# Moving an offset shift from TensorE to four small transfers, with norm and offset convolution one step earlier

## The chip, the cores and the metric

The kernel runs on one core of a Trainium2 chip. The metric is the time of one execution in microseconds (us). TensorE (PE) multiplies matrices, and its weight loads are listed apart (PEld); VectorE is DVE, ScalarE is ACT, GpSimd is POOL; SyncE (SP) issues transfers, and so does ACT's queue here (SPq and ACTq in the profile).

## The reference, cut to what matters

The program is two "metaformer" layers on x of 4 images, 128 channels, 128 x 128 pixels. Only the first part is touched here, a deformable 3 x 3 convolution of the channel-normalised input:

```python
offset = _offset_conv(x, w_off)                 # 3x3 convolution, 18 channels: dy, dx of 9 taps
py = base_y.astype(x.dtype)[None] + dy
px = base_x.astype(x.dtype)[None] + dx
sampled = _bilinear_gather(x, py, px)
return jnp.einsum('bckhw,ock->bohw', sampled, w_conv.reshape(O, C, K * K))
...
x = x + _L0_conv_ref(_ln_c(x), L0_conv_w_off, L0_conv_w_conv)
```

The rest (two expert layers, a spectral convolution) is the same in both kernels.

## The kernel before, in words

`phase_a` computes this convolution. A group G is four image rows; there are 128 groups (`NG`). `order_a` writes out by hand, in slots, a list of stages that all engines walk through in the same order, each picking its own stages. A step s is 12 slots (18 at the end of an image, where six rows instead of four are sampled). In one step the stages belong to different groups: F = s+4 is loaded, transposed and normalised and gets its offset convolution, Z = s+2 gets its offsets, N = s+1 its bilinear weights, a quad of four rows is sampled, and s-2 gets the output convolution. The names that matter:

- `turn` (PE, L350) transposes the group's rows into PSUM bank 4; `stats` (DVE, L496 and L499) takes mean and variance from there; `scale` (POOL, L562 to L568) makes the scale and bias `rs`; `norm` (ACT, L437) writes the normalised rows `a_tn`; `norm_out` (ACT's queue, L446) sends them to memory, from where SP fetches windows `a_win`.
- `conv` (PE, L361) multiplies by the offset weights into banks 5 and 6, two rows at a time (`h` 0 and 1); `y_out` (ACT, L464) scales the result into the ring `a_yr`, with four activations or five, five where rows wrap in the ring.
- `zsum` (POOL, L589, L595) adds over the three tap rows and gives `a_zz` with three tap columns; `shift` (PE, L374) moves the outer tap columns by one pixel, which is one partition, by multiplying with two shift matrices into bank 6; `offs` (DVE, L517) adds the middle column and writes the offsets `a_on`.
- `offs_out` (ACT's queue, L450) stores them; `place` and `hats` (POOL, L623 or L631, L607, L610) spread them; `bend` (ACT, L473), `clip` (DVE, L528), `prod` (DVE L536, POOL L576) and `turn_s` (DVE, L545) make the weights `a_tt`.
- `sample` (PE, L405) multiplies windows by weights in three thirds. The first and the last third write banks 0 to 3, the second writes banks 4 to 7. So before the second third PE waits until norm, stats, y_out, offs and residual have read what these banks held:

```python
w.wait_ge(normed, convs)
w.wait_ge(mv_ready, convs // 2)
w.wait_ge(y_ready, 2 * convs)
w.wait_ge(on_ready, shifts)
w.wait_ge(x1_ready, outs)
```

- `evict` (ACT L482, DVE L509) copies each third out; `out` (PE, L423) is the output convolution in nine taps; `residual` (DVE, L551) adds the input.

POOL takes the stages of a step in the order prod, zsum, prod, place, hats, scale. ACT takes the three evicts, offs_out, bend, norm, norm_out, y_out. Each engine does its own in that order whatever is ready.

Of the kernel before, what the change touches and what calls it, by code (L numbers as in the profile page):

```python
# [46 lines left out]
def setup_phase(nc, ctx, ins, k):  # L47
# [5 lines left out]
    with nc.Block() as block:  # L53
# [17 lines left out]
        @block.sync  # L71
        def _(e):
            e.dma_start(k["wraw"][:, :], ins["wof"][:, :]).then_inc(w_in, 16)
            e.dma_start(k["ident"][:, :], ins["ident"][:, :]).then_inc(loaded, 16)
            e.dma_start(k["shift"][:, :, :], ins["shift"][:, :, :]).then_inc(loaded, 16)
# [3 lines left out]
            e.wait_ge(loaded, 80)  # L79
            e.wait_ge(w_in, 16)  # L80
# [10 lines left out]
NX, NTN, NYR, NOC = 10, 3, 12, 32  # L91
# [69 lines left out]
def order_a():  # L161
# [16 lines left out]
    end = t0  # L178
    for s in range(-4, NG + 3):
        t0 = steps[s]  # L180
        F, Z, N = s + 4, s + 2, s + 1
        if s == -4:
            for G in range(3):
                put(t0, "load", G)
            put(t0, "border", 0)
# [4 lines left out]
        if 3 <= s + 7 < NG:  # L190
            put(t0 + 6, "load", s + 7)
# [9 lines left out]
        if 0 <= Z < NG:  # L201
            put(t0 + 4, "shift", Z)
            put(t0 + 4, "offs", Z)
        if 0 <= F < NG:
            put(t0 + 4, "turn", F)
            put(t0 + 4, "stats", F)
            put(t0 + 6, "scale", F)
            put(t0 + 5, "conv", F, 0)
            put(t0 + 6, "conv", F, 1)
            put(t0 + 7, "norm", F, 0)  # L210
# [33 lines left out]
def phase_a(nc, ctx, ins, k, xtp, offd, x1d):  # L244
# [6 lines left out]
    zz = S("a_zz", [128, 2, 4, 3, 18])  # L251
# [12 lines left out]
    OF = SB[:, 6, 324:396].rearrange("p (r f) -> p r f", r=4)  # L264
# [4 lines left out]
    def sem(name):  # L269
# [4 lines left out]
    turned, convolved, shifted, sampled, conv_out = (  # L274
        sem(n) for n in ("turned", "convolved", "shifted", "sampled", "conv_out"))
# [3 lines left out]

    filled, bn_done, mv_ready, on_ready, reached, clipped, weighed_dve, turned_s, x1_ready = (  # L280
# [51 lines left out]
    def tensor(e):  # L332
        w = Once(e)

        convs = shifts = outs = taken = 0
# [6 lines left out]
        for o in order:  # L342
# [9 lines left out]
            elif o[0] == "conv":  # L352
# [3 lines left out]
                if h:  # L356

                    w.wait_ge(on_ready, shifts)
# [5 lines left out]
            elif o[0] == "shift":  # L364
                G = o[1]
                bank_free()
                w.wait_ge(z_step, z_count[G])

                w.wait_ge(on_ready, G)
                w.wait_ge(y_ready, 2 * convs)  # L370
                shifts += 1

                for kx in (0, 2):
                    t = e.matmul(OF[:, :, :], k["shift"][:, kx, :], zz[:, G % 2, :, kx, :], start=(kx == 0),  # L374
                                 stop=(kx == 2))
                t.then_inc(shifted, 1)
            elif o[0] == "sample":
# [8 lines left out]
                for h in range(3):  # L386
                    if h == 1:
# [4 lines left out]
                        w.wait_ge(on_ready, shifts)  # L392
# [36 lines left out]
    def scalar(e):  # L429
        w = Once(e)  # L430
        for o in order:
# [20 lines left out]
            elif o[0] == "y_out":  # L452
                _, G, h = o
                b, q = divmod(G, GI)
                for r in (2 * h, 2 * h + 1):
# [12 lines left out]
                    a.then_inc(y_ready, 1)  # L468
            elif o[0] == "bend":
# [15 lines left out]
    def vector(e):  # L485
        w = Once(e)
        e.memset(oc[:, :], 0.0)
        e.memset(sx[:, :, :, :], 0.0)
        e.memset(tt[:, :, 2304:2306], 0.0).then_inc(filled, 1)
        for o in order:  # L490
# [20 lines left out]
            elif o[0] == "offs":  # L511
                G = o[1]
                w.wait_ge(shifted, G + 1)
# [3 lines left out]
                e.tensor_tensor(on[:, G % 2, :, :], OF[:, :, :], zz[:, G % 2, :, 1, :], ALU.add).then_inc(on_ready, 1)  # L517
# [35 lines left out]
    def gpsimd(e):  # L553
        w = Once(e)
        for o in order:
# [24 lines left out]
            elif o[0] == "zsum":  # L580
                G = o[1]
                q = G % GI
                v = yr[:, 4 * G % NYR * 162:(4 * G % NYR + 4) * 162].rearrange("p (r k f) -> p r k f", r=4, k=3)
                z = zz[:, G % 2, :, :, :].rearrange("p r k f -> p r (k f)")
# [1187 lines left out]
def program(nc, ins, out, dbg):  # L1772
    with ExitStack() as ctx:
# [38 lines left out]
def constants():  # L1812
    ident = np.eye(128, dtype=np.float32)
    shift = np.zeros((128, 3, 128), np.float32)
    for kx in range(3):
        x = np.arange(max(0, 1 - kx), min(128, 129 - kx))
        shift[x + kx - 1, kx, x] = 1.0
# [20 lines left out]
    return {"io": io, "pick": pick, "rev": rev, "ident": ident, "shift": shift, "cx": np.ascontiguousarray(cx), "cy": np.ascontiguousarray(cy), "base": base, "far": far}  # L1838
# [41 lines left out]
```

## Time and profile before

| | us |
|---|---|
| median of 3 runs | 3873.46 (3870.35 to 3874.3) |
| profiled execution, its own time | 3877.71 |
| its span, first to last instruction | 3875.7 |
| PE busy | 3679.2 (95%) |
| DVE busy | 2944.7 (76%) |
| ACT busy | 1570.9 (41%) |
| POOL busy | 1474.4 (38%) |

The mean granted TensorE clock was 0.956 of full speed. The span is the time between the first and the last instruction of the profile; the profiled execution is one of several, so its time differs a little from the median. Phase A ends near 1990 us of the span; a busy share says nothing of who is waited for, so the rows further down are taken from single steps of that phase. Overlapping matmuls are counted once in a busy time.

### The profile page before, as it was taken

The numbers are of one execution on the slowest core, as the hardware profiler recorded it, in microseconds if no ns is written. First come the engines' busy times: TensorE is split into PE (matmuls) and PEld (weight loads), VectorE is DVE, ScalarE is ACT, GpSimd is POOL, SyncE is SP. The second block draws the span as 40 slices with busy tenths as digits, with TensorE's granted clock in tenths as the row PEclk, the third lists the DMA queues.
The fourth block names the chain that finished last, engine by engine and source line by source line (L and its number), as shares of the span: only waits on it lengthen the run. The fifth ranks groups of instructions, "written<-read, shape, count | busy, mean of one in ns | idle before, by whom it ended". The sixth has DMA issues, their size and how long they took to land. (4 is left out here: it accounts for less than half of the span.)

```text
span 3875.7 us, 89814 instructions
## 1 busy us (share of the span) xinstructions
PE 3679.2 (95%) x31511; PEld 2470.7 (64%) x31511; DVE 2944.7 (76%) x9687; ACT 1570.9 (41%) x4565; POOL 1474.4 (38%) x2661
## 2 busy tenths in 40 slices
PE   6999999999999999999979999999999999996667
PEld 5777777777777777777745666666666666654444
DVE  4666666666666666666648999999999999996633
ACT  3444444444444444444411444434343443434224
POOL 4444444444454444444412333333333333333210
PEclk7999999999999999999979999999999999997755
DMA  5655555555555555555527777777777777884789
GB/s 109 108 95 108 100 95 97 96 108 104 91 99 95 108 103 94 96 97 97 88 81 265 270 275 274 272 268 273 277 271 275 267 276 273 285 303 158 268 312 393
DMA packets 611250, 709.81 MB, mean 183 GB/s; under 512 B 62208, under 2 KB 493824, under 8 KB 594416
## 3 DMA queue, kind: packets, MB, share of 16 engines
q1 hardware_dynamic: 505328, 630.10, 58.3%
q10 hardware_dynamic: 104448, 71.85, 6.0%
q8 instruction: 253, 4.15, 0.5%
q14 instruction: 197, 1.61, 0.2%
q0 software_dynamic: 1024, 2.10, 0.2%
HBM read 521.26 MB, written 181.50 MB: 181 GB/s over the span
## 5 line engine op out<-in xcount | busy, mean ns | idle before, releaser
L423 PE MATMUL a_sb<-a_sr,wcv 128*128 128x512 f32 (+3 forms) x2820 | 1052.2, 515 | 0.8 <-DVE a_xo L551 0.8
L405 PEld LDWEIGHTS a_sb<-a_tt,a_win 32*128 32x128 f32 x19008 | 647.0, 186 | 116.3 <-issue 115.5
L423 PEld LDWEIGHTS a_sb<-a_sr,wcv 128*128 128x128 f32 x2820 | 493.1, 190 | 333.9 <-issue 289.1
L405 PE MATMUL a_sb<-a_tt,a_win 32*128 32x144 f32 x19008 | 679.8, 295 | 17.5 <-ACT a_yr L464 11.0
L1171 DVE TENSOR_TENSOR b_P<-b_P,b_x 128x1024 f32<-128x1024 f32 x512 | 620.1, 1212 | 0.0
L509 DVE COPY a_sr<-a_sb 128x432 f32<-128x432 f32 (+14 forms) x1172 | 419.6, 413 | 204.1 <-PE a_sb L405 204.0
L482 ACT COPY a_sr<-a_sb 128x432 f32<-128x432 f32 (+14 forms) x1172 | 362.9, 389 | 356.4 <-PE a_sb L405 356.4
L1074 PE MATMUL b_z<-b_P,b_ew 128*128 128x512 f32 x1024 | 463.4, 596 | 0.0
L1077 PE MATMUL b_z<-b_P,b_ew 128*128 128x512 f32 x1024 | 460.3, 592 | 0.0
L1300 POOL TENSOR_TENSOR b_ss<-b_st 128x12 f32<-128x12 f32 (+2 forms) x139 | 29.9, 215 | 1050.6 <-DVE b_pp L1245 963.5
L545 DVE STREAM_TRANSPOSE a_tt<-a_sx 128x576 f32<-128x576 f32 x520 | 398.7, 768 | 14.2 <-POOL a_sx L576 5.4
L576 POOL TENSOR_TENSOR a_sx<-a_hh 128x576 f32<-128x576 f32 x260 | 307.5, 1183 | 126.7 <-DVE a_tt L545 123.3
L551 DVE TENSOR_TENSOR a_xo<-a_sb,a_xin 128x512 f32<-128x512 f32 x128 | 88.4, 691 | 345.3 <-PE a_sb L423 345.3
L1077 PEld LDWEIGHTS b_z<-b_P,b_ew 128*128 128x128 f32 x1024 | 194.7, 190 | 194.0 <-issue 187.9
L1074 PEld LDWEIGHTS b_z<-b_P,b_ew 128*128 128x128 f32 x1024 | 189.2, 195 | 185.2 <-issue 185.2
L1316 POOL TENSOR_TENSOR b_rs<-b_ss,mhalf 128x12 f32<-128x12 f32 (+2 forms) x139 | 302.0, 2172 | 11.1 <-POOL b_ss L1312 0.4
L437 ACT ACTIVATE a_tn<-a_sb,a_rs 128x128 f32<-128x128 f32 x512 | 192.4, 456 | 216.8 <-POOL a_rs L568 216.8
L473 ACT ACTIVATE a_hh<-a_hh 128x576 f32<-128x576 f32 (+1 forms) x128 | 88.3, 690 | 462.8 <-POOL a_hh L610 462.8
L1144 ACT ACTIVATE c_tn<-c_x,b_rs 128x128 f32<-128x128 f32 x512 | 163.7, 390 | 242.1 <-POOL b_rs L1316 242.1
L464 ACT ACTIVATE a_yr<-a_sb,zero,a_rs 128x162 f32<-128x162 f32 (+2 forms) x594 | 226.5, 467 | 57.0 <-ACT a_tn L437 57.0
L623 POOL COPY a_oc<-a_on 128x72 f32<-128x72 f32 x112 | 29.0, 259 | 548.7 <-DVE a_on L517 548.7
L361 PEld LDWEIGHTS a_sb<-wof,a_xin 128*128 128x128 f32 x1024 | 170.7, 195 | 85.3 <-issue 58.1
(186 smaller groups left out, 5374.3 us busy)
## 6 DMA issues: line engine op xcount, KB each, us to landing
b_P<-pd SPq DMA_DIRECT2D x128, 2048.0 KB, 7.8
a_win<-xtp SPq DMA_DIRECT2D x2144, 36.0 KB
a_xin<-in_x SPq DMA_DIRECT2D x128, 256.0 KB, 6.0
xtp<-a_tn ACTq DMA_DIRECT2D x128, 256.0 KB, 2.3
x1d<-a_xo SPq DMA_DIRECT2D x128, 256.0 KB, 5.7
b_x<-x1d SPq DMA_DIRECT2D x128, 256.0 KB, 7.7
x2d<-b_xa SPq DMA_DIRECT2D x128, 256.0 KB, 3.5
pw<-x3d SPq DMA_DIRECT2D x128, 256.0 KB, 6.6
```

Source lines behind the costliest of these rows:

```text
L405: t = e.matmul(d[:, 0:3 * m_, :, NU_ * i:NU_ * i + NU_], win[32 * q:32 * q + 32, half_of(Q, j) % NWH, NWIN // 3 * h + i, :], m, start=(j = ...
L423: t = e.matmul(ob[:, r:r + m, :], k["wcv"][:, 3 * (2 - kr) + kx, :], rows[:, :, t_, :], start=(t_ == 0 and r == 0), stop=(t_ == 8))
L437: a = e.activation(tn[:, G % NTN, r, :], TK[:, r, :], ACT.Identity, bias=rs[:, G % 2, r:r + 1], scale=rs[:, G % 2, 4 + r:5 + r])
L464: a = e.activation(yr[:, d:d + 216 * m].rearrange("p (k f) -> p k f", f=216)[:, :, 0:54], YB[r // 2][:, r % 2, 54 * kr:54 * (kr + m)].rear ...
L482: a = e.copy(d, v)
L509: a = e.tensor_copy(d, v)
L545: e.transpose(tt[:, Q % NTP, 0:2304].rearrange("p (j a t x) -> p a t j x", j=2, a=4, t=9)[:, n - quad(Q)[0]], sx[:, n % NST, :, :].rearran ...
L576: e.tensor_tensor(sx[:, n % NST, :, 0:NI * NJ].rearrange("p t (j i) -> p t j i", j=NJ), hh[:, G % 2, i, :, None, 0:NI].to_broadcast([128, ...
L1074: e.matmul(ZE[u][:, :, :], ew[:, x, :], P[:, G % NPB, :, x, :], start=(x == 0), stop=False)
L1077: e.matmul(ZE[u][:, :, :], ew[:, x, :], P[:, G % NPB, :, x, :], start=False, stop=False)
L1171: t = e.tensor_tensor(v, v, x1[:, G % NX1, r, None, :].to_broadcast([128, 8, 128]), ALU.mult)
L1316: e.tensor_tensor(rs[:, u, c], ss[:, u, 2, c], k["mhalf"][:, c], ALU.pow).then_inc(scaled, 1)
```

## The change

The shift of the outer tap columns leaves PE: ACT's queue now issues four transfers from `a_zz` to a new buffer `a_zs`, 112 and 15 partitions for each of the two columns, into one partition higher or lower. `offs` becomes two dependent additions on DVE, both from SBUF. The offsets' group is Z = s+2 as before, but `zsum` and `shift` are now done for M = s+3, and load, turn, stats, scale, norm, conv and y_out for F = s+5; so the loop begins one step earlier (s = -5) and the ring of input rows has 11 places instead of 10. In the list `offs` stands behind `turn` and `stats` of the same slot, where it stood ahead of them. The last of the nine matmul windows of `sample` writes two tap columns of two positions instead of three of four. PE no longer waits for `on_ready`, neither ahead of the second `conv` nor ahead of the second third of `sample`. The constant `shift` and its load go away.

```diff
-    for s in range(-4, NG + 3):
+    for s in range(-5, NG + 3):
-        F, Z, N = s + 4, s + 2, s + 1
+        F, M, Z, N = s + 5, s + 3, s + 2, s + 1
...
-        if 0 <= Z < NG:
-            put(t0 + 4, "shift", Z)
-            put(t0 + 4, "offs", Z)
         if 0 <= F < NG:
             put(t0 + 4, "turn", F)
             put(t0 + 4, "stats", F)
...
+        if 0 <= M < NG:
+            put(t0 + 1, "zsum", M)
+            put(t0 + 4, "shift", M)
         if 0 <= Z < NG:
-            put(t0 + 1, "zsum", Z)
+            put(t0 + 4, "offs", Z)
             put(t0 + 5, "offs_out", Z)
...
-                if h:
-
-                    w.wait_ge(on_ready, shifts)
...
-                for kx in (0, 2):
-                    t = e.matmul(OF[:, :, :], k["shift"][:, kx, :], zz[:, G % 2, :, kx, :], start=(kx == 0),
-                                 stop=(kx == 2))
-                t.then_inc(shifted, 1)
...
-                        w.wait_ge(on_ready, shifts)
...
+                                t0, nx = (1, 2) if 3 * h + i == NWIN - 1 else (0, NU_)
+                                m = bass.AP(m.tensor, m.offset + 31 * t0,
+                                            [list(m.ap[0]), [96, 3 * m_], [31, 3 - t0], [1, nx]])
...
+            elif o[0] == "shift":
+                G = o[1]
+                w.wait_ge(z_step, z_count[G])
+                w.wait_ge(filled, 1)
+                w.wait_ge(on_ready, G - 1)
+                for p, n in ((0, 112), (112, 15)):
+                    e.dma_start(zs[p + 1:p + n + 1, G % 2, 0, :, :], zz[p:p + n, G % 2, 0, :, :]
+                                ).then_inc(shifted[G % 2], 16)
+                    e.dma_start(zs[p:p + n, G % 2, 1, :, :], zz[p + 1:p + n + 1, G % 2, 2, :, :]
+                                ).then_inc(shifted[G % 2], 16)
...
-                w.wait_ge(shifted, G + 1)
+                w.wait_ge(shifted[G % 2], 64 * (G // 2 + 1))
+                w.wait_ge(z_step, z_count[G])
...
-                e.tensor_tensor(on[:, G % 2, :, :], OF[:, :, :], zz[:, G % 2, :, 1, :], ALU.add).then_inc(on_ready, 1)
+                e.tensor_tensor(on[:, G % 2, :, :], zs[:, G % 2, 0, :, :], zz[:, G % 2, 1, :, :], ALU.add
+                                ).then_inc(on_half, 1)
+                w.wait_ge(on_half, G + 1)
+                e.tensor_tensor(on[:, G % 2, :, :], on[:, G % 2, :, :], zs[:, G % 2, 1, :, :], ALU.add
+                                ).then_inc(on_ready, 1)
```

DVE in the middle of phase A, from the first product of a step (`prod`, L536) on: before,

```order
L536 TENSOR_TENSOR a_sx<-a_hh 128x576
L545 STREAM_TRANSPOSE a_tt<-a_sx 128x9x2x32
L517 TENSOR_TENSOR a_on<-a_sb,a_zz 128x72
L496 BN_STATS a_st<-a_sb 128x6 x4
L499 BN_AGGR a_mv<-a_st 128x2 x4
L545 STREAM_TRANSPOSE a_tt<-a_sx 128x9x2x32
L522 TENSOR_REDUCE fm<-a_on 128x1
```

and now, where `prod` is L538 and `turn_s` L547:

```order
L538 TENSOR_TENSOR a_sx<-a_hh 128x576
L547 STREAM_TRANSPOSE a_tt<-a_sx 128x9x2x32
L493 BN_STATS a_st<-a_sb 128x6 x4
L496 BN_AGGR a_mv<-a_st 128x2 x4
L515 TENSOR_TENSOR a_on<-a_zs,a_zz 128x72
L518 TENSOR_TENSOR a_on<-a_on,a_zs 128x72
L547 STREAM_TRANSPOSE a_tt<-a_sx 128x9x2x32
```

The offsets (`a_on`) are one addition ahead of the eight instructions of `stats` before, and two additions behind them now.

PE at the same place, from the last output taps of a step over the sampling (`a_win`) to the next output tap: before,

```order
L423 MATMUL a_sb<-a_sr,wcv 128x512 x3
L405 MATMUL a_sb<-a_tt,a_win 128x36x4 x72
L374 MATMUL a_sb<-a_zz,shift 128x72 x2
L350 MATMUL a_sb<-ident,a_xin 128x128 x4
L423 MATMUL a_sb<-a_sr,wcv 128x512
L361 MATMUL a_sb<-wof,a_xin 128x162 x2
```

and now, where sampling is L391, the transpose L351, the output taps L409 and the offset convolution L359:

```order
L409 MATMUL a_sb<-a_sr,wcv 128x512 x3
L391 MATMUL a_sb<-a_tt,a_win 128x36x4 x64
L391 MATMUL a_sb<-a_tt,a_win 128x12x2x2 x8
L351 MATMUL a_sb<-ident,a_xin 128x128 x4
L409 MATMUL a_sb<-a_sr,wcv 128x512
L359 MATMUL a_sb<-wof,a_xin 128x162 x2
```

The shift is gone, and eight of the 72 matmuls of the sampling are narrower. (In the trace each of these matmuls is two instructions.)

ACT from the last copy of a sampled third to the norm: before,

```order
L482 COPY a_sr<-a_sb 128x4x3x2x10
L450 DMA offd<-a_on 128x72
L473 ACTIVATE a_hh<-a_hh 128x576
L437 ACTIVATE a_tn<-a_sb,a_rs 128x128 x4
```

and now, where these are L478, L436, L469 and L423:

```order
L478 COPY a_sr<-a_sb 128x4x3x2x10
L461 DMA a_zs<-a_zz 112x72
L463 DMA a_zs<-a_zz 112x72
L461 DMA a_zs<-a_zz 15x72
L463 DMA a_zs<-a_zz 15x72
L436 DMA offd<-a_on 128x72
L469 ACTIVATE a_hh<-a_hh 128x576
L423 ACTIVATE a_tn<-a_sb,a_rs 128x128 x4
```

Four issues stand ahead of the store of the offsets and of everything behind it.

## Rows read from the trace of the kernel before

**Rows 1.** Busy times by stage: us, then each engine's busy us (instructions).
```profile
core 0: us, PE busy (x) PEld busy (x) DVE busy (x) ACT busy (x) POOL busy (x), PEclk, DMA share, GB/s
...
600.00:1100.00 500.00, 498.25 (x6154) 359.48 (x6153) 339.50 (x934) 224.34 (x620) 242.15 (x396) 1.00 0.55 99
```

**Rows 2.** Waits of 100 to 1900 us: total, times, longest.
```profile
PE a_sb L405 <- DVE a_sr L509: 2.8, 3, 0.9
...
PE a_sb L405 <- ACT a_yr L464: 1.6, 2, 0.8
```

**Rows 3.** Timeline of PE: start, duration, engine and line.
```profile
1088.29 5.09 PE L405 MATMUL a_sb<-a_tt,a_win 32*128 32x144 f32 x144
1093.31 0.67 PE L374 MATMUL a_sb<-a_zz,shift 128*128 128x72 f32 x4
1093.81 0.60 PE L350 MATMUL a_sb<-ident,a_xin 128*128 128x128 f32 x4
...
1103.17 5.09 PE L405 MATMUL a_sb<-a_tt,a_win 32*128 32x144 f32 x144
...
1311.75 5.10 PE L405 MATMUL a_sb<-a_tt,a_win 32*128 32x144 f32 x144
...
1401.14 5.10 PE L405 MATMUL a_sb<-a_tt,a_win 32*128 32x144 f32 x144
```

**Rows 4.** Timeline of DVE in the same step.
```profile
1095.82 0.19 DVE L517 TENSOR_TENSOR a_on<-a_sb,a_zz 128x72 f32<-128x72 f32 x1
1095.93 0.88 DVE L496 BATCH_NORM_STATS2 a_st<-a_sb 128x6 f32<-128x128 f32 x4
1096.73 0.35 DVE L499 BATCH_NORM_AGGREGATE a_mv<-a_st 128x2 f32<-128x6 f32 x4
1097.00 0.74 DVE L545 STREAM_TRANSPOSE a_tt<-a_sx 128x576 f32<-128x576 f32 x1
```

**Rows 5.** Timelines of POOL, then ACT, same step.
```profile
1096.08 0.24 POOL L623 COPY a_oc<-a_on 128x72 f32<-128x72 f32 x1 [5.05 <-DVE a_on L517]
...
1099.90 0.19 POOL L568 TENSOR_SCALAR a_rs<-a_rs 128x4 f32<-128x4 f32 x1
...
1096.04 0.36 ACTq L450 DMA_DIRECT2D offd<-a_on  x1
...
1102.08 1.62 ACT L464 ACTIVATE a_yr<-a_sb,zero,a_rs 128x162 f32<-128x162 f32 x4 [0.44 <-ACT a_tn L437]
```

**Rows 6.** Timelines of ACT and PE where PE waited for ACT.
```profile
494.36 1.86 ACT L464 ACTIVATE a_yr<-a_sb,zero,a_rs 128x54 f32<-128x54 f32 x5 [0.44 <-ACT a_tn L437]
...
496.47 3.50 PE L405 MATMUL a_sb<-a_tt,a_win 32*128 32x144 f32 x96 [0.77 <-ACT a_yr L464]
499.90 0.67 PE L374 MATMUL a_sb<-a_zz,shift 128*128 128x72 f32 x4
```

**Rows 7.** A longer step on PE and ACT; then two groups, by line.
```profile
1078.38 0.67 PE L374 MATMUL a_sb<-a_zz,shift 128*128 128x72 f32 x4
...
1087.62 1.86 ACT L464 ACTIVATE a_yr<-a_sb,zero,a_rs 128x54 f32<-128x54 f32 x5 [0.45 <-ACT a_tn L437]
...
L464 ACT ACTIVATE a_yr<-a_sb,zero,a_rs 128x162 f32<-128x162 f32 (+2 forms) x594 | 226.5, 467 | 57.0 <-ACT a_tn L437 57.0
...
L631 POOL COPY a_oc<-a_on 128x12 f32<-128x12 f32 (+3 forms) x80 | 11.6, 195 | 80.6 <-DVE a_on L517 80.6
```

**Rows 8.** Timeline of PE, sampling of 72 columns.
```profile
524.64 4.26 PE L405 MATMUL a_sb<-a_tt,a_win 32*128 32x72 f32 x144
```

**Rows 9.** Store of the offsets, ACT queue, all 128 issues.
```profile
DMA to landing us min/median/max: 2.8/5.5/8.3
```

**Rows 10.** Timeline of PE at the start.
```profile
10.25 1.12 PE L350 MATMUL a_sb<-ident,a_xin 128*128 128x128 f32 x4 [6.42 <-DMA a_xin<-in_x]
...
16.29 0.79 PE L350 MATMUL a_sb<-ident,a_xin 128*128 128x128 f32 x4 [2.85 <-ACT a_tn L437]
...
59.21 5.78 PE L405 MATMUL a_sb<-a_tt,a_win 32*128 32x144 f32 x96 [3.46 <-ACT a_yr L464]
```

More of the change, by code:

```diff
@@ L78, in _ @@
             e.dma_start(k["cy"][:, :, :], ins["cy"][:, :, :]).then_inc(loaded, 16)
-            e.wait_ge(loaded, 80)
+            e.wait_ge(loaded, 64)
             e.wait_ge(w_in, 16)
@@ L90 @@
 NU_, NWIN = 4, 9
-NX, NTN, NYR, NOC = 10, 3, 12, 32
+NX, NTN, NYR, NOC = 11, 3, 12, 32
 NST, NTP, NWH, NSR = 2, 3, 4, 12
@@ L178, in order_a @@
     end = t0
-    for s in range(-4, NG + 3):
+    for s in range(-5, NG + 3):
         t0 = steps[s]
-        F, Z, N = s + 4, s + 2, s + 1
-        if s == -4:
+        F, M, Z, N = s + 5, s + 3, s + 2, s + 1
+        if s == -5:
             for G in range(3):
@@ L189, in order_a @@
             put(t0 + 6, "border", s // GI + 1)
-        if 3 <= s + 7 < NG:
-            put(t0 + 6, "load", s + 7)
+        if 3 <= s + 8 < NG:
+            put(t0 + 6, "load", s + 8)
         if 0 <= N < NG:
@@ L206, in order_a @@
             put(t0 + 4, "stats", F)
-            put(t0 + 6, "scale", F)
             put(t0 + 5, "conv", F, 0)
             put(t0 + 6, "conv", F, 1)
+            put(t0 + 6, "scale", F)
             put(t0 + 7, "norm", F, 0)
@@ L250, in phase_a @@
     yr = S("a_yr", [128, NYR * 162 + 216])
-    zz = S("a_zz", [128, 2, 4, 3, 18])
+    zz = S("a_zz", [128, 2, 3, 4, 18])
+    zs = S("a_zs", [128, 2, 2, 4, 18])
     on = S("a_on", [128, 2, 4, 18])
@@ L271, in sem @@
         return sems[-1]
-    turned, convolved, shifted, sampled, conv_out = (
-        sem(n) for n in ("turned", "convolved", "shifted", "sampled", "conv_out"))
+    turned, convolved, sampled, conv_out = (
+        sem(n) for n in ("turned", "convolved", "sampled", "conv_out"))
+    shifted = [sem(f"shifted{i}") for i in range(2)]
     normed, y_ready, bent, taken_act = (sem(n) for n in ("normed", "y_ready", "bent", "taken_act"))
     taken_dve = sem("taken_dve")
+    on_half = sem("on_half")
     filled, bn_done, mv_ready, on_ready, reached, clipped, weighed_dve, turned_s, x1_ready = (
@@ L333, in tensor @@
         w = Once(e)
-        convs = shifts = outs = taken = 0
+        convs = outs = taken = 0
         def bank_free():
@@ L363, in tensor @@
                 t.then_inc(convolved, 1)
[L364 to L371, printed above, removed]
-                for kx in (0, 2):
-                    t = e.matmul(OF[:, :, :], k["shift"][:, kx, :], zz[:, G % 2, :, kx, :], start=(kx == 0),
-                                 stop=(kx == 2))
-                t.then_inc(shifted, 1)
             elif o[0] == "sample":
@@ L488, in vector @@
         e.memset(sx[:, :, :, :], 0.0)
+        e.memset(zs[:, :, :, :, :], 0.0)
         e.memset(tt[:, :, 2304:2306], 0.0).then_inc(filled, 1)
@@ L582, in gpsimd @@
                 q = G % GI
-                v = yr[:, 4 * G % NYR * 162:(4 * G % NYR + 4) * 162].rearrange("p (r k f) -> p r k f", r=4, k=3)
-                z = zz[:, G % 2, :, :, :].rearrange("p r k f -> p r (k f)")
+                v = yr[:, 4 * G % NYR * 162:(4 * G % NYR + 4) * 162].rearrange("p (r k x f) -> p r k x f", r=4, k=3, x=3)
+                z = zz[:, G % 2, :, :, :].rearrange("p x r f -> p r x f")
                 n = z_count[G]
@@ L1789, in program @@
             SA = lambda name, shape, dt=F32: ca.enter_context(nc.sbuf_tensor(name, shape, dt))
-            k |= {"zero": SA("zero", [128, 640]), "wof": SA("wof", [128, 162]), "shift": SA("shift", [128, 3, 128]), "wcv": SA("wcv", [128, 9, 128]),
+            k |= {"zero": SA("zero", [128, 640]), "wof": SA("wof", [128, 162]), "wcv": SA("wcv", [128, 9, 128]),
                   "cx": SA("cx", [128, 9, NI]), "cy": SA("cy", [128, 14, NJ])}
@@ L1813, in constants @@
     ident = np.eye(128, dtype=np.float32)
[L1814 to L1817, printed above, removed]
     x, t, i = np.arange(128)[:, None, None], np.arange(9)[None, :, None], np.arange(NI)[None, None, :]
@@ L1837, in constants @@
     rev = np.ascontiguousarray(ident[:, (128 - np.arange(128)) % 128])
-    return {"io": io, "pick": pick, "rev": rev, "ident": ident, "shift": shift, "cx": np.ascontiguousarray(cx), "cy": np.ascontiguousarray(cy), "base": base, "far": far}
+    return {"io": io, "pick": pick, "rev": rev, "ident": ident, "cx": np.ascontiguousarray(cx), "cy": np.ascontiguousarray(cy), "base": base, "far": far}
 OUTN = ["out"]
```

5 lines of the change are left out of this document (1 added, 4 removed).

## The prediction

> **What bounds the kernel now.** I first read the busy times by stage. In 500 us of phase A PE is busy for 498.25 us at full clock, with DVE at 339.50 [rows 1]. Next the waits: over 1800 us the sampling matmuls stood for DVE 2.8 us and for ACT 1.6 us in all [rows 2]. So before the change PE is the bound, and whatever leaves PE is a gain, if nothing else sets the period then. Six sampling starts from 1311.75 to 1401.14 give (1401.14 - 1311.75)/6 = 14.90 us a step [rows 3].
>
> The question is how far behind the next chain is. PE stops ahead of the second third of sampling until y_out has emptied the banks. That chain starts at E, the end of the last third, which I take as the start of what follows it on PE (1093.31, the shift [rows 3]). In the step from there:
>
> - DVE does its copies, a product and a turn, then the offsets at 1095.82 (E+2.51), ready at 1096.01 (E+2.70), then stats, which hold DVE to 1097.00 [rows 4].
> - POOL has waited 5.05 us for the offsets when it starts at 1096.08; it spreads them, makes the hats, and only behind these the scale, which ends at 1100.09 [rows 5]. Stats had ended at 1097.08 [rows 4]: the scale is late because of the offsets ahead of it on POOL, not of its own input.
> - ACT then norms and scales; y_out ends at 1102.08 + 1.62 = 1103.70, E+10.39 [rows 5].
>
> PE starts the next sampling at 1103.17 [rows 3]. What lies between the second third's start and the next E is seen where PE did wait: y_out ended at 494.36 + 1.86 = 496.22, the first of 96 matmuls started at 496.47 (0.25 later), and E came at 499.90, 3.43 after it [rows 6]. So y_out's end to E is 3.68 us when the wait binds. In the step above the second third started at about 1103.17 + (5.02 - 3.43) = 1104.76 (5.02 is 1093.31 - 1088.29), and the chain would have allowed 1103.95. **The slack is only 0.81 us** in a step with four activations, 0.24 less where y_out has five (1.86 against 1.62 [rows 5, 7]), and in the longer step E = 1078.38, y_out end 1089.48, it is E+11.10 [rows 7], a slack of some 0.1.
>
> **The change part by part.**
>
> *Shift off PE.* Shift to transpose is 1093.81 - 1093.31 = 0.50 us [rows 3]. Gain on PE: 0.50 a step.
>
> *Narrower last window.* 144 sampling matmuls of 72 columns take 4.26 us, of 144 columns 5.09 [rows 3, 8]: 29.6 against 35.3 ns each, so halving the columns saves a sixth, not a half; something else than columns is near. Eight matmuls of two instructions narrow from 144 to 48 columns: 16 x 5.7 ns = 0.09 us a step. If the slope went on below 72 columns it were 0.12, if it stopped at once 0. I take 0.09.
>
> *Waits for on_ready gone.* The first, ahead of the second conv, is not among PE's waits of note; the second was met long before. Worth 0. The chain through y_out stays, since PE still waits for it.
>
> *Offsets behind stats, and two additions.* This is the part that decides. DVE reaches this point at E+2.51 as before (its copies, product and turn are untouched, and the transposes that stats need are done 0.50 earlier). Stats occupy 1097.00 - 95.93, that is 1.07 us [rows 4]. Then the first addition 0.19 and, as it waits for its own engine's result, the second 0.19 + 0.04 (bounds for this pair's extra: 0.1 if it overlaps as the four stats do, 0.35 if the wait costs 0.15). The offsets are ready 1.07 + 0.23 = **1.30 us later against E**. Behind them on POOL stand place, hats and scale, all in a row without idle time; behind these norm and y_out. Earlier statistics help nothing, the scale is not waiting for them. POOL was idle for 5.05 us in front of the offsets, so it can't have anything to catch up with.
>
> By the Trainium skill (VectorE: DVE Perf Modes, the section on the TRN2 errata) an operation that reads PSUM has 120 fixed cycles and one that reads SBUF 58, so an addition from SBUF would be 0.06 us shorter than the one with a PSUM operand; an estimate from that page is 0.13 us less delay and about 16 us off the total. The trace has 0.19 for the addition with one operand in PSUM [rows 4] and none with both in SBUF. The sum does not use it.
>
> *Four issues on ACT's queue.* One issue takes 0.36 [rows 5]; four are 1.44. ACT issues the store of the offsets at 1096.04, 0.03 after they are ready [rows 4, 5], so whatever it has to do first is done by E+2.73. With four issues ahead it is there at E+4.17 at the latest, and the offsets come at E+4.00 now: at most 0.17 late for the store, and bend behind it waits for POOL's hats anyway, norm for the scale at E+8.1. Hidden. Their wait for zsum was met a step ago. Landing of the similar store is 2.8 to 8.3 us [rows 9], and there is a step of 15 us for it: hidden too. Were the cover gone, it would be a further delay of the same chain.
>
> *One step more of fill.* Without sampling a step is about 6 us: 16.29 - 10.25 [rows 10]; part of it runs while the windows are still loading. I take +3 (0 to 7). In return one step that lacks transpose and conv is no longer bound by the chain at the end: with the shift-free steps there, -4.
>
> **The sum.** PE alone: 14.90 - 0.50 - 0.09 = 14.31. Chain: y_out end E+10.39 + 1.30 = 11.69, then 3.68 - 0.09 = 3.59, together 15.28. Of 594 activations 82 are beyond four a step [rows 7]: 0.24 x 82/128 = +0.15. The 80 small copies are five in each of 16 steps [rows 7], which cost 11.10 - 10.39 - 0.24 = 0.47 each: +0.06. Period 15.49, so the chain sets it, PE idles 1.2 us in each step, and a step is 0.59 longer than now. Over the 123 steps that sample and norm: +73. Five steps were bound by this chain already (three with six rows, one of them in rows 6, and two at the start, one the 3.46 us wait [rows 10]): these get 0.6 more each, +3. With fill and end: 73 + 3 + 3 - 4 = **+75 us**. On the profiled execution's 3877.71 (span 3875.7 and 2.0 around it) that is 3953. The median of the runs is 4.3 lower than that execution, so I forecast 3948.
>
> **The rivals.**
>
> *PE stays the bound.* If the delay did not reach PE, each step would be 0.59 shorter: -75 us, with the fill 3802. For it: PE's 99.7% in rows 1. Against: it needs 1.30 + 0.59 = 1.89 us of slack, and 0.81 is there.
>
> *The additions are nearly free in the chain.* Were only the second addition late (0.23, as when stats did not stand in front), the chain were 14.42 a step: -0.48, 3877.71 - 59 + 2, less 4.3: 3816. The point at which the sign turns is a delay of 1.30 - 0.59 = 0.71 us. Against it: the order of the DVE rows, where stats stand ahead. In between, no change.
>
> *The clock falls.* PE idles 1.2 us in each step. After a wait of 3.46 us at the start the 96 matmuls took 5.78 [rows 10] against 3.50 after one of 0.77 [rows 6]. If the longer wait brought the lower of the two levels (1.2 GHz instead of 2.4), up to 2.3 us a step would be added: 3948 + 280 = 4230 at most, less if only some steps have it. Against: 1.2 is nearer to 0.77, and PE is busy for the other 14 us. The Trainium skill (TensorE: Matmul & The Clock Gate, part 1) says that activity releases the throttle and an idle spell brings it back; that would be this rival.
>
> *The shifted columns arrive late* or the issues hold up ACT: at three times the price the issues would end at E+7.1, store and bend behind them would run into norm at E+8.1, and 0.1 to 0.4 us a step is 3960 to 4000. For it speaks only that this transfer is not in the trace.
>
> **How the numbers follow.** Chain-bound 82%, PE-bound 6%, chain with little delay 4% (and between the two signs 2%), clock 4%, ACT's queue 2%. Bounds of the sum: release of PE at 0.1 instead of 0.25 (-0.13), the pair at 0.1 (-0.13) give -32 us; the pair at 0.35, no gain from the window and a fill of 7 give +30. The range is 3914 to 3975. A difference over 0.2% (8 us) can be told from none: faster 0.10, same 0.02, slower 0.88.
>
> **What would show it.** In the profile after: PE waiting for ACT's y_out in nearly every step, some 150 us in all, where it was 1.6; sampling starts 15.3 to 15.7 us apart; POOL's place starting at E+4.1 instead of E+2.77; y_out ending near E+11.7; stats ahead of two additions; no shift on PE; the clock still 1.00 in the middle. The forecast is wrong if place starts at E+3, or if sampling starts are 14.3 apart, or if PE waits for something else than y_out.

## The result and the profile after

The changed kernel takes 3966.77 us (median of 4 runs, 3961.83 to 3974.75), the kernel before 3872.43 beside it: a ratio of 1.0246 (95% interval 1.0226 to 1.0266), so 94 us slower. Forecast were 3948 us and +75. The profiled execution took 3970.15 (span 3968.1, mean granted clock 0.952).

I read it in the order of the prediction. First the busy time by stage of the kernel after (us, then each engine's busy us and instructions, PEclk, DMA share, GB/s):

```profile
600.00:1100.00 500.00, 467.23 (x5697) 333.30 (x5695) 333.09 (x927) 209.39 (x589) 227.40 (x372) 0.99 0.50 98
```

PE was busy for 498.25 of these 500 us [rows 1] and is for 467.23: it now idles, and the granted clock is nearly 1 all the same. Every other engine has less to do as well, since fewer steps fit into 500 us. Who PE waits for is in the waits of 100 to 1900 us (total, times, longest):

```profile
POOL a_oc L625 <- DVE a_on L518: 625.2, 99, 8.2
...
PE a_sb L391 <- ACT a_yr L450: 113.5, 114, 2.7
```

The wait for ACT's y_out was 1.6 us in 2 cases [rows 2]; now it comes in 114 steps and is 113.5 us long in all. The waits of sampling for DVE are as they were, 2.8 us in 3 cases. POOL still sits idle for 6 us before the offsets and can't have been the bottleneck by its amount of work, only by its place in the chain.

One step on PE, kernel after (start, duration):

```profile
1086.99 1.88 PE L391 MATMUL a_sb<-a_tt,a_win 32*128 32x144 f32 x48
...
1090.00 3.33 PE L391 MATMUL a_sb<-a_tt,a_win 32*128 32x144 f32 x96 [1.12 <-ACT a_yr L450]
1093.26 0.66 PE L351 MATMUL a_sb<-ident,a_xin 128*128 128x128 f32 x4
...
1102.71 1.89 PE L391 MATMUL a_sb<-a_tt,a_win 32*128 32x144 f32 x48
...
1105.30 3.34 PE L391 MATMUL a_sb<-a_tt,a_win 32*128 32x144 f32 x96 [0.69 <-ACT a_yr L450]
1108.57 0.66 PE L351 MATMUL a_sb<-ident,a_xin 128*128 128x128 f32 x4
```

The end of the last third is followed at once by the transpose (L351): the shift [rows 3] is gone. Sampling, which stood as one block of 144 matmuls, is split at its second third by the wait. E = 1093.26 in this step, the next is 1108.57: 15.31 us, where the kernel before had 14.90 [rows 3]. The same step on DVE:

```profile
1095.04 0.78 DVE L547 STREAM_TRANSPOSE a_tt<-a_sx 128x576 f32<-128x576 f32 x1
1095.74 0.85 DVE L493 BATCH_NORM_STATS2 a_st<-a_sb 128x6 f32<-128x128 f32 x4
1096.52 0.35 DVE L496 BATCH_NORM_AGGREGATE a_mv<-a_st 128x2 f32<-128x6 f32 x4
1096.84 0.23 DVE L515 TENSOR_TENSOR a_on<-a_zs,a_zz 128x72 f32<-128x72 f32 x1
1097.10 0.23 DVE L518 TENSOR_TENSOR a_on<-a_on,a_zs 128x72 f32<-128x72 f32 x1
```

Against E: the turn ends at E+2.56, stats take until E+3.6, the additions until E+4.07. Before, the offsets were ready at E+2.70 [rows 4]. What follows on POOL and ACT (ACTq is the queue of ACT's DMA issues):

```profile
1097.40 0.25 POOL L625 COPY a_oc<-a_on 128x72 f32<-128x72 f32 x1 [6.31 <-DVE a_on L518]
...
1101.24 0.19 POOL L570 TENSOR_SCALAR a_rs<-a_rs 128x4 f32<-128x4 f32 x1
```

```profile
1093.39 0.62 ACTq L461 DMA_DIRECT2D a_zs<-a_zz  x1
1094.05 0.61 ACTq L463 DMA_DIRECT2D a_zs<-a_zz  x1
1094.69 0.86 ACTq L461 DMA_DIRECT2D a_zs<-a_zz  x1
1095.58 0.86 ACTq L463 DMA_DIRECT2D a_zs<-a_zz  x1
...
1097.37 0.83 ACTq L436 DMA_DIRECT2D offd<-a_on  x1
...
1103.42 1.62 ACT L450 ACTIVATE a_yr<-a_sb,zero,a_rs 128x162 f32<-128x162 f32 x4 [0.45 <-ACT a_tn L423]
```

Place starts at E+4.14, scale ends at E+8.17, y_out ends at 1105.04 = E+11.78, and PE's 96 matmuls start 0.26 after that. Each link is later by the delay of the offsets and by nothing else: from place's start to y_out's end it is 7.64 us, before 1103.70 - 1096.08 = 7.62 [rows 5].

**Where the 94 us lie.** I took E, the end of the last third, in every step of both traces. From the first sampling step to the last that also transposes there are 122 steps. In 15 of them POOL's place is made of several small copies (the "small copies" of the prediction); three of these are among the four steps in the fifth row:

| | before, us | after, us | difference |
|---|---|---|---|
| E of the first sampling step | 48.48 | 59.10 | +10.6 |
| 103 steps without small copies | | | +59.2 (0.574 each) |
| 12 steps with small copies | | | +13.5 (1.13 each) |
| 3 steps with the extra quad (ends of images) | 60.77 | 68.61 | +7.8 |
| 4 steps (three with six rows of y among them) | 61.81 | 70.41 | +8.6 |
| end of phase A | | | -2.7 |
| the rest of the program | | | -4.6 |

Together, to rounding, +92.4, the difference of the spans. By kind, as medians: a step with four activations of y_out went from 14.93 to 15.32, one with five from 14.88 to 15.55. The two step lengths came out within 0.04 of the forecast; the surplus is in the fill and in seven exceptional steps.

The same from PE's side is in the group of sampling by line, over the whole run of the kernel after (busy us, mean ns of one, idle us just before and what ended it):

```profile
L391 PE MATMUL a_sb<-a_tt,a_win 32*128 32x144 f32 (+1 forms) x19008 | 702.8, 297 | 143.6 <-ACT a_yr L450 133.4 <-issue 6.5 <-DVE a_sr L506 2.8
```

In the kernel before this group was busy for 679.8 us, with 17.5 idle ahead of it. So 126.1 us of idle time and 23.0 of busy time came on. Against them stands the shift: in the step from 1093.31 the first output tap followed the shift's start by 0.94, and now it follows E by 0.49, so 0.45 a step, or 55 us in 123 steps. That is +94 from this group alone; idle time of other groups in the fill and the rest of the program are not in it. The busy time rose though the window is narrower because a sampling split by a wait is dearer than one block (1.89 + 3.34 = 5.23 against 4.95 of the same matmuls unsplit in experiment 3 below); the clock adds some at a few places.

### The profile page after: what moved, and what is told of

It reads as the page before. It is cut to its first block and busy times, and to the rows that moved or that the text cites. A ratio compares the mean times of both kernels' runs of the same rounds, so it can differ in the third digit from the quotient of the medians.

```text
span 3968.1 us, 89430 instructions
## 1 busy us (share of the span) xinstructions
PE 3644.7 (92%) x30999; PEld 2424.4 (61%) x30999; DVE 2986.8 (75%) x9816; ACT 1559.0 (39%) x4565; POOL 1471.2 (37%) x2661
## 5 line engine op out<-in xcount | busy, mean ns | idle before, releaser
L409 PE MATMUL a_sb<-a_sr,wcv 128*128 128x512 f32 (+3 forms) x2820 | 1052.1, 515 | 0.8 <-DVE a_xo L553 0.8
L391 PE MATMUL a_sb<-a_tt,a_win 32*128 32x144 f32 (+1 forms) x19008 | 702.8, 297 | 143.6 <-ACT a_yr L450 133.4
L391 PEld LDWEIGHTS a_sb<-a_tt,a_win 32*128 32x128 f32 x19008 | 659.7, 189 | 266.2 <-issue 265.7
L409 PEld LDWEIGHTS a_sb<-a_sr,wcv 128*128 128x128 f32 x2820 | 492.9, 190 | 335.0 <-issue 289.9
L478 ACT COPY a_sr<-a_sb 128x432 f32<-128x432 f32 (+14 forms) x1172 | 364.8, 396 | 287.5 <-PE a_sb L391 287.5
L547 DVE STREAM_TRANSPOSE a_tt<-a_sx 128x576 f32<-128x576 f32 x520 | 402.0, 774 | 14.2 <-POOL a_sx L578 5.4
L469 ACT ACTIVATE a_hh<-a_hh 128x576 f32<-128x576 f32 (+1 forms) x128 | 88.3, 690 | 638.6 <-POOL a_hh L612 638.6
L423 ACT ACTIVATE a_tn<-a_sb,a_rs 128x128 f32<-128x128 f32 x512 | 192.8, 456 | 219.0 <-POOL a_rs L570 215.2
L359 PEld LDWEIGHTS a_sb<-wof,a_xin 128*128 128x128 f32 x1024 | 171.4, 196 | 83.4 <-issue 76.5
L530 DVE TENSOR_SCALAR a_hh<-a_hh 128x576 f32<-128x576 f32 (+1 forms) x128 | 59.5, 465 | 211.9 <-ACT a_hh L469 211.9
```

The costliest lines, as they stand in the source:

```text
L391: t = e.matmul(d[:, 0:3 * m_, t0:3, NU_ * i:NU_ * i + nx], win[32 * q:32 * q + 32, half_of(Q, j) % NWH, NWIN // 3 * h + i, :], m, start=(j ...
L409: t = e.matmul(ob[:, r:r + m, :], k["wcv"][:, 3 * (2 - kr) + kx, :], rows[:, :, t_, :], start=(t_ == 0 and r == 0), stop=(t_ == 8))
L423: a = e.activation(tn[:, G % NTN, r, :], TK[:, r, :], ACT.Identity, bias=rs[:, G % 2, r:r + 1], scale=rs[:, G % 2, 4 + r:5 + r])
L478: a = e.copy(d, v)
L547: e.transpose(tt[:, Q % NTP, 0:2304].rearrange("p (j a t x) -> p a t j x", j=2, a=4, t=9)[:, n - quad(Q)[0]], sx[:, n % NST, :, :].rearran ...
```

## The experiments

The theory: the offsets are 1.3 us later because stats stand ahead of them on DVE, and the one chain from them to y_out carries that to PE in each step. Rivals still to be told apart from it: the four transfers (their issues or their landing) cost the time, or idle PE slows by its clock.

**1. The offsets ahead of the statistics (offs_first).** This alone is undone of the order; transfers and additions stay:

```diff
+        if 0 <= Z < NG:
+            put(t0 + 4, "offs", Z)
         if 0 <= F < NG:
...
         if 0 <= Z < NG:
-            put(t0 + 4, "offs", Z)
             put(t0 + 5, "offs_out", Z)
```

> The changed kernel with one thing undone: on DVE the two additions of offs stand ahead of stats again, as before the change. Theory (the offsets behind stats lengthen the chain through POOL and y_out that PE waits for): the delay of the offsets falls from 1.33 to about 0.26 us, the chain to 10.39 + 0.26 + 3.59 = 14.24 us for a step with four activations (so PE's own 14.31 decides there), 14.48 with five; sampling starts 14.3 to 14.5 us apart, time about 3966 - 122 x 1.08 = 3835 (3820 to 3850), faster than the kernel before. Rival (PE loses its time to something else the change brought, the transfers on ACT's queue or the clock): the order of two stages on DVE does not matter, the time stays at 3950 to 3970.

Measured: 3832.39 us (3829.42 to 3835.74, 3 timed runs and the profiled one), ratio to before 0.9893 (0.9878 to 0.9908), as the theory expected and 118 us and more under the rival. Moving one stage in the list turns 94 us slower into 41 us faster, a swing of 134 us. DVE, ACT's y_out, then PE of this kernel, in the step with E = 1090.95:

```profile
1093.43 0.19 DVE L516 TENSOR_TENSOR a_on<-a_zs,a_zz 128x72 f32<-128x72 f32 x1
1093.66 0.23 DVE L519 TENSOR_TENSOR a_on<-a_on,a_zs 128x72 f32<-128x72 f32 x1
1093.81 0.88 DVE L494 BATCH_NORM_STATS2 a_st<-a_sb 128x6 f32<-128x128 f32 x4
```

```profile
1099.96 1.86 ACT L451 ACTIVATE a_yr<-a_sb,zero,a_rs 128x54 f32<-128x54 f32 x5 [0.45 <-ACT a_tn L424]
```

```profile
1085.94 5.07 PE L392 MATMUL a_sb<-a_tt,a_win 32*128 32x144 f32 x144
1090.95 0.66 PE L352 MATMUL a_sb<-ident,a_xin 128*128 128x128 f32 x4
...
1100.36 5.05 PE L392 MATMUL a_sb<-a_tt,a_win 32*128 32x144 f32 x144
1105.34 0.66 PE L352 MATMUL a_sb<-ident,a_xin 128*128 128x128 f32 x4
```

The offsets are ready at E+2.94, 0.24 later than before the change; the sampling of a step is one block again, and sampling starts are 1100.36 - 1085.94 = 14.42 apart. In 100 to 1900 us PE waits 10.9 us for y_out, in 16 cases, and in the middle of phase A it is busy for 495.11 of 500 us. A busy PE is not the whole story here: y_out, with five activations, ends at 1101.82 = E+10.87, and with the 0.26 to PE's start and 3.27 from there to E (both as in the kernel after) the chain gives 14.40 for this step, which took 14.39. The sampling, 5.05 long where it is 4.95 without any wait (experiment 3), has the short wait inside it. So steps with five activations (median 14.42) are now at the chain's own length, and only those with four (median 14.34, chain 14.17) are set by PE: the two are level. This is also the fastest version of the study, together with experiment 5, which it can't be told from.

**2. One addition (one_add).** The second addition and the wait ahead of it go; this kernel leaves the right-hand tap column out of the offsets.

```diff
                 e.tensor_tensor(on[:, G % 2, :, :], zs[:, G % 2, 0, :, :], zz[:, G % 2, 1, :, :], ALU.add
-                                ).then_inc(on_half, 1)
-                w.wait_ge(on_half, G + 1)
-                e.tensor_tensor(on[:, G % 2, :, :], on[:, G % 2, :, :], zs[:, G % 2, 1, :, :], ALU.add
                                 ).then_inc(on_ready, 1)
```

> The changed kernel without the second addition of offs: the right-hand tap column is left out of the offsets, stats still stand in front. Theory: every step is set by the chain, so the 0.26 us of the addition and its wait come off each of 122 steps one for one: 3966 - 32 = 3934 (3925 to 3943). Rival (PE or the transfers set the step): no change, 3966, or within 5 us of it.

Measured: 3931.09 us (3928.60 to 3934.47), ratio 1.0148 (1.0132 to 1.0163): 35.7 us under the kernel after, where 32 were expected. PE of this kernel:

```profile
1089.78 0.66 PE L351 MATMUL a_sb<-ident,a_xin 128*128 128x128 f32 x4
...
1101.77 3.36 PE L391 MATMUL a_sb<-a_tt,a_win 32*128 32x144 f32 x96 [0.69 <-ACT a_yr L450]
1105.06 0.65 PE L351 MATMUL a_sb<-ident,a_xin 128*128 128x128 f32 x4
```

This step (y_out in five activations) is 15.28 long and the one with four 15.04, against 15.55 and 15.32 in the kernel after: some 0.28 us, one short DVE operation off the chain, comes off every step. PE does the same work and ACT's queue issues the same four transfers in both, so the chain sets the period, not PE.

**3. The narrow window alone, on the kernel before (before_narrow).**

```diff
+                                t0, nx = (1, 2) if 3 * h + i == NWIN - 1 else (0, NU_)
+                                m = bass.AP(m.tensor, m.offset + 31 * t0,
+                                            [list(m.ap[0]), [96, 3 * m_], [31, 3 - t0], [1, nx]])
```

> The kernel before with the narrower last window alone (eight matmuls of 72 write 48 instead of 144 columns). Theory: 0.09 us a step on a PE that is the bound, 132 samplings: -12 us, 3860 (3857 to 3872). If the narrow matmuls cost as much as wide ones: 3872. If they cost in proportion to columns (35.3 ns down to 12 ns, 16 of them): -0.37 a step, 3823.

Measured: 3856.04 us (3851.92 to 3857.87), ratio 0.9953 (0.9940 to 0.9967): -16.4 us against 3872.45, the kernel before measured beside it. The theory had 12 and a range down to 3857: the measured gain lies just beyond it. PE of this kernel:

```profile
1082.31 4.95 PE L407 MATMUL a_sb<-a_tt,a_win 32*128 32x144 f32 x144
1087.19 0.67 PE L374 MATMUL a_sb<-a_zz,shift 128*128 128x72 f32 x4
...
1097.05 4.97 PE L407 MATMUL a_sb<-a_tt,a_win 32*128 32x144 f32 x144
```

Sampling takes 4.95 instead of 5.09, the step 14.74 instead of 14.90. So the gain is 0.15 a step and not 0.09. Sixteen matmuls save 9.4 ns each for 96 columns, 0.10 ns per column, where 144 against 72 columns gave 5.7 ns, 0.08 per column: the price doesn't flatten below 72 columns. While PE is the bound each 0.1 us a step on it is worth about 12 us; in the changed kernel the same edit sits in the 3.33 us between y_out and E.

**4. No step between the transfer and its use (no_lead).** Norm and offset convolution go back to where they stood, zsum and the transfers into the step of the offsets. The transfers then stand in the chain.

```diff
-    for s in range(-5, NG + 3):
+    for s in range(-4, NG + 3):
...
-        F, M, Z, N = s + 5, s + 3, s + 2, s + 1
+        F, M, Z, N = s + 4, s + 2, s + 2, s + 1
```

> The changed kernel without the step of lead: F = s+4, zsum and the transfers for s+2 as the offsets (ten input rows again), the order on DVE as in the changed kernel. Theory: the additions then wait for four issues (0.61, 0.61, 0.86, 0.86 us) and a landing of some 4 us in their own step, about E+6.5 instead of E+3.6, and every step is 2.9 us longer: 18.4 us, time 3966 + 125 x 2.9 = 4330 (4200 to 4450). Rival (the transfers would have landed in time without the lead): 3950 to 3966.

Measured: 4815.49 us (4810.61 to 4820.38, 1 timed run and the profiled one), ratio 1.2434 (1.2411 to 1.2456), granted clock 0.88. The direction was right, the size far off, outside the stated range. DVE, then PE, in the step with E = 1076.62, then the middle of phase A:

```profile
1085.18 0.23 DVE L515 TENSOR_TENSOR a_on<-a_zs,a_zz 128x72 f32<-128x72 f32 x1 [4.94 <-DMA a_zs<-a_zz]
```

```profile
1094.39 5.55 PE L391 MATMUL a_sb<-a_tt,a_win 32*128 32x144 f32 x96 [6.04 <-ACT a_yr L450]
```

```profile
600.00:1100.00 500.00, 370.07 (x4039) 276.31 (x4039) 228.38 (x643) 146.96 (x422) 160.22 (x262) 0.85 0.40 68
```

The expectation reckoned with a wait for the transfers on DVE, and it is there (4.94). But the last of the four issues ends at 1079.77 (E+3.15) and the first addition starts only at 1085.18, so the offsets are ready at 1085.68, E+9.06, where E+6.5 was expected: 5.0 us later than in the kernel after, not 2.9. The rest is the clock: PE stands 6.04 us for y_out, and the 96 matmuls after that take 5.55 instead of 3.33. This step (with small copies) is 23.25 long, where such a step takes 16.1 in the kernel after. So the extra step of lead in the change is not a luxury: it keeps the transfers out of the chain. And it shows that the clock rival becomes real once nearly every step has a long wait: 0.85 is granted in the middle of phase A.

**5. The fill in another order (fill_first).** To win back the fill, in the steps before sampling the scale stands ahead of place and hats on POOL, bend behind y_out on ACT, the offsets behind stats; the rest is experiment 1.

```diff
-        if 0 <= Z < NG:
+        if 0 <= Z < NG and s >= 0:
             put(t0 + 4, "offs", Z)
...
-            put(t0 + 6, "scale", F)
+            put(t0 + (6 if s >= 0 else 4), "scale", F)
...
-            put(t0 + 6, "bend", Z)
+            put(t0 + (6 if s >= 0 else 10), "bend", Z)
```

> offs_first with another order in the steps before sampling begins (s < 0) alone: POOL's scale stands ahead of place and hats, ACT's bend behind y_out, and offs behind stats on DVE. Theory (the start is late because norm and offset convolution of the groups ahead stand behind the first offsets, whose transfers land 8 us after issue beside the first window loads): PE's wait of 4.3 us ahead of the second third of the first sampling goes, the first transpose after it moves from 56.8 to about 52, and the total falls by about 5 us: 3827 (3823 to 3831). Rival (the first sampling is late because of its own offsets and windows, and the next steps are set by the chain anyway): 3830 to 3834, no change.

Measured: 3834.31 us (3829.65 to 3836.25), ratio 0.9891 (0.9874 to 0.9907): no gain over experiment 1, so my theory missed. PE at the start of this kernel:

```profile
52.31 1.89 PE L394 MATMUL a_sb<-a_tt,a_win 32*128 32x144 f32 x48 [1.27 <-ACT a_yr L453]
...
57.19 2.00 PE L394 MATMUL a_sb<-a_tt,a_win 32*128 32x144 f32 x48 [3.00 <-DVE a_sr L509]
...
59.12 1.11 PE L354 MATMUL a_sb<-ident,a_xin 128*128 128x128 f32 x4
```

The wait for y_out did shrink, from 4.33 in experiment 1 to 1.27, but a new one came behind it, 3.00 for DVE's evictions (L509), and the first sampling step ends at 59.12, while it ended at 56.76 in experiment 1. The rival's number fits, but it named neither the evictions nor why they are late. The trace has that link on DVE:

```profile
52.77 0.46 DVE L533 TENSOR_SCALAR a_hh<-a_hh 128x576 f32<-128x576 f32 x1 [4.89 <-ACT a_hh L472]
```

POOL's hats are ready at 50.19, but ACT's bend stands behind y_out now and starts at 52.04. DVE's clip, above, waits for it, and behind the clip stand a product and two turns, so the evictions start only at 55.79. The new order took a wait off one chain and put it on another.

**6. Two transfers of 127 partitions (two_of_127).** Experiment 1 with one transfer per direction in place of 112 and 15 rows:

```diff
-                for p, n in ((0, 112), (112, 15)):
+                for p, n in ((0, 127),):
...
-                w.wait_ge(shifted[G % 2], 64 * (G // 2 + 1))
+                w.wait_ge(shifted[G % 2], 32 * (G // 2 + 1))
```

> offs_first with two transfers of 127 partitions instead of four of 112 and 15. Theory (a full step lies between issue and use): the transfer may land later, but no step waits for it, so the time is that of offs_first, 3832, within 5 us. Rival: 127 rows land more slowly than the room of some 12 us, DVE waits for them in each step, and the time rises by 122 x the excess, 3900 and more.

Measured: 3919.77 us (3914.14 to 3924.15), ratio 1.0110 (1.0093 to 1.0127): 87 us more than with four. Neither theory nor rival saw how. ACT and its queue in one of the worst steps, then two waits of 100 to 1900 us, then the store of the offsets over all 128 groups (duration of an issue in ns, min/median/max):

```profile
1077.36 2.94 ACTq L464 DMA_DIRECT2D a_zs<-a_zz  x1
1080.34 6.54 ACTq L437 DMA_DIRECT2D offd<-a_on  x1
...
1086.93 0.68 ACT L470 ACTIVATE a_hh<-a_hh 128x576 f32<-128x576 f32 x1 [9.41 <-issue]
```

```profile
ACT a_hh L470 <- issue: 498.8, 78, 12.7
...
PE a_sb L392 <- ACT a_yr L451: 63.1, 53, 7.2
```

```profile
L437 ACTq DMA_DIRECT2D offd<-a_on x128: 338/3614/7462, 41.4 to 1985.4; - x128
```

DVE waits for the columns in only 2 cases, 17.1 us in all. Nor do the two issues cost the time: together they have a median of 1.64 us, less than the 2.93 of the four (the 2.94 above is one of ten over 2 us). What costs is the issue of the store of the offsets behind them: a median of 3.61 us, up to 7.46, where experiment 1 has 0.55 and at most 0.97. ACT's bend, a link of the chain to the turned samples, stands behind it in 78 cases for 498.8 us; y_out's part of this reaches PE as 63.1 us of waits (10.9 in experiment 1). Over the whole run the sampling group has 95.8 us idle ahead of it and 697.5 busy, in experiment 1 33.7 and 676.8: 83 of the 87 us. The Trainium skill (DMA: Bandwidth & Descriptors, "Why a DMA increments its semaphore by 16 and not by 1") says that the number of DMA engines for a transfer is the largest one up to 16 that divides the outermost dimension, so 127 partitions go to a single engine while 112 can use 16. That would fit the blocked queue, but it is not shown: no view here tells the DMA engines apart, and no run tried a third way to split the rows.

## Why the prediction was right, point by point

*PE was the bound with only 0.81 us behind it.* Right. With 0.24 us more delay than before (experiment 1) PE and the chain are level, with the 1.37 of the change PE waits in 114 steps.

*Shift off PE, 0.50; narrower window, 0.09.* Both were mis-sized. The window gives 0.15 (experiment 3). The shift gives 0.45: from its start to the first output tap it was 0.94 [rows 3 and the tap at 1094.25], from E to that tap it is 0.49 now; start to start, as the prediction took it, leaves out that the transposes behind a shift take 0.05 less. Steps with four activations say the same: 14.93 before, 14.78 in experiment 3, 14.34 in experiment 1, so 0.15 and 0.44. The two errors cancel: 0.59 was forecast and 0.59 measured, which is luck.

*Offsets 1.30 later.* Measured E+4.07 against E+2.70: 1.37. Stats put the first addition at E+3.58, as forecast. The additions take 0.23 each with both operands in SBUF, not 0.19, and 0.49 from the start of the first to the end of the second (0.42 forecast); the 0.04 for the wait between them, an assumption, is 0.03 in the step above. The estimate from the Trainium skill (VectorE: DVE Perf Modes, the section on the TRN2 errata), by which an addition from SBUF is 0.06 us shorter than one with an operand in PSUM, is not borne out: 0.19 with PSUM [rows 4], 0.23 or 0.19 here without. The measurement decides, and leaving it out of the sum was right.

*The chain period.* Forecast 15.28 (four activations), 15.52 (five), 15.99 (small copies), measured 15.32, 15.55 and, as the mean of twelve, 16.08. The extra 0.07 of delay and the 0.06 too little for the window nearly cancel, which is luck; the mechanism is not: each of the links (place E+4.14 against E+4.1, y_out E+11.78 against 11.69) is where the sum put it. The forecast +0.59 is a mean with the small copies spread over all steps. Without them it is +0.53, and the 103 steps without small copies show +0.574. PE's waits for y_out, some 150 us forecast, are 133.4 over the whole run; sampling in two pieces costs PE another 0.28 a step, and that part of the gap counts as busy.

*ACT's queue costs nothing.* Right in its result, wrong in its price. The four issues take 0.62 + 0.61 + 0.86 + 0.86 = 2.95, not 1.44, twice what one issue of the store suggested [rows 5]. The cover was enough even so: the last ends at E+3.18, still ahead of the offsets at E+4.07. In experiment 1, with the offsets at E+2.94, that cover is gone, and the store issues at 1094.22, 0.33 after they are ready, since the fourth transfer's issue ends only at 1094.18.

*Landing hidden.* Right in the steady state. From issue to landing, for the first and the second direction of the kernel after:

```profile
DMA to landing us min/median/max: 2.2/2.9/10.2
```

```profile
DMA to landing us min/median/max: 2.6/4.2/11.2
```

*Fill +3.* **This term failed in size**: E of the first sampling step is 10.6 us later. DVE, then PE, at the start of the kernel after:

```profile
35.72 0.23 DVE L515 TENSOR_TENSOR a_on<-a_zs,a_zz 128x72 f32<-128x72 f32 x1 [4.37 <-DMA a_zs<-a_zz]
```

```profile
42.08 1.09 PE L351 MATMUL a_sb<-ident,a_xin 128*128 128x128 f32 x4 [9.25 <-ACT a_tn L423]
...
46.78 3.26 PE L391 MATMUL a_sb<-a_tt,a_win 32*128 32x144 f32 x48 [0.71 <-DVE a_tt L547]
...
54.21 4.95 PE L391 MATMUL a_sb<-a_tt,a_win 32*128 32x144 f32 x96 [4.17 <-ACT a_yr L450]
```

I took half of the extra step as hidden beside the loads. The transposes of the fill start at 10.25, 16.29, 25.00 and 34.54 before, and at 10.15, 16.19, 21.72, 29.06 and 42.08 now: the step more costs 5.5 us, the one behind it is 1.4 shorter, and the last one is 13.0 long where it was 9.5. In that one the first addition stands 4.37 us for the transfers, because the steps of the fill are short and the step of lead that hides the transfers later doesn't hide them here; the transpose behind it stands 9.25 for the norm. That makes 7.5 of the 10.6; the other 3 lie between that transpose and E, and were not taken apart. That the window loads under way made the first landings slow (their maximum is 10 to 11 us) is likely but was not separated.

*Exceptional steps.* The sum gave +0.59 to every step and 0.6 more to five that already waited for y_out, three of them with six rows. (Two such waits are in [rows 2]; the third of these steps, 14.97 long before, had none.) The three steps with the extra quad got 7.8 where the sum has 1.8, and four more, the three with six rows and one with small copies, 8.6 where it has 4.2: 10.4 us too much. The fill adds 7.6, the end 1.3 (-2.7 where -4 was forecast) and the rest of the steps between 3 and 4; the rest of the program gives back 4.6. That accounts, within 1 us, for the 17 us by which the span exceeds the forecast. A part of the exceptional steps is clock (next point); the remainder was not taken apart.

*The rivals.* PE as the bound: refuted by the waits in 114 steps and by experiment 2. (The slack that it would need is 1.80 and not 1.89, since the narrower window shortens the chain too; nothing hangs on it.) Additions nearly free: this is experiment 1's order, 3832 where the rival said 3816. ACT's queue: no for the change, yes in experiment 6. The clock: refuted as the main cause, since the ordinary step's 96 matmuls take 3.33 after waits of about 1 us, but not absent. PE of the kernel after, at two such places, the second at the end of an image:

```profile
784.12 4.84 PE L391 MATMUL a_sb<-a_tt,a_win 32*128 32x144 f32 x96 [1.77 <-ACT a_yr L450]
```

```profile
561.88 6.98 PE L391 MATMUL a_sb<-a_tt,a_win 32*128 32x144 f32 x144 [0.96 <-DVE a_sr L506]
```

The second of these took 5.26 in the kernel before (at 529.83), with the wider window and the same kind of wait. The granted clock there is 0.83 from 555 to 562 us and then:

```profile
562.00:570.00 8.00, 7.96 (x151) 7.79 (x152) 5.44 (x30) 3.44 (x27) 1.18 (x1) 0.72 0.58 69
```

So part of the time runs at the lower of the two levels (1.2 GHz) there. It costs 1.7 us in this step and 1.5 in each of two others (784.12, and one at 1541.46 after a wait of 2.24): some 5 us of the 94.

*The range.* The lower bound fits 0.15 for the earlier release of PE (0.25 to 0.1), not the 0.13 written beside it; the upper terms, +30, would give 3978 where 3975 stands. The measured 3966.77 is inside either way, in the upper part, which is where the fill and the exceptional steps put it.

What stays open: the 4.6 us less in the rest of the program, and what beside the clock lengthens each exceptional step.

## What to carry to other kernels

When one engine is 99.7% busy, first measure how far behind it the next chain is. Here it was 0.81 us in a step of 14.9, and so a gain of 0.59 on PE could only be kept whole if nothing in that chain moved by more than some 0.4 (0.1 in a step with five activations). An edit that takes work off the bound and pays for it with later operands elsewhere has to be reckoned in the chain: the same work with one stage in another place of the list was 134 us apart.

A queue on an engine that also computes is part of its program: count the issues by their own durations, and look at what stands behind them. And a step of lead hides a transfer only if the step is long enough: the 15 us of a full step were enough here, the short steps of the fill were not.

## What the runs showed of the hardware

- One DMA issue on ACT's queue took 0.36 us for the store of the kernel before [rows 5], and in the kernel after 0.37 as a median and 0.83 at most for the same store; 0.61 for 112 partitions from SBUF to SBUF, 0.86 for 15 partitions (medians of 256 each), and 0.63 and 1.01 for the first and the second transfer of 127 (medians of 128; the second up to 5.50). Fewer rows were not cheaper to issue.
- Behind two transfers of 127 partitions the issue of the store on the same queue took a median of 3.61 us and up to 7.46 (experiment 6), where behind four of 112 and 15 it took 0.55 and at most 0.97 (experiment 1).
- A float32 addition of 72 elements with both operands in SBUF took 0.19 or 0.23 us, no less than with one operand in PSUM (0.19).
- The granted clock fell after some waits of PE and not after others: 4.84 and 4.87 us for 96 matmuls after waits of 1.77 and 2.24, but 3.36 after waits of 2.36 (526.75) and 2.65 (1035.68) in the same kernel, and 5.55 after 6.04 in experiment 4. The length of the last wait alone doesn't tell it.
- Sampling matmuls of 48 instead of 144 columns save 0.15 us in 16, 9 ns each (experiment 3). A sampling that is split by a wait is 0.28 us longer on PE than one in a single block (5.23 against 4.95), the wait itself not counted.
